# Moving the 128x64 block-mask add of an attention kernel from GpSimd to VectorE

## The chip, the cores and the metric

The kernel runs as one program on the 8 cores of one Trainium2 chip. Each core takes 2 of the 16 sequences (2048 tokens each, 1024 channels) and works for itself; the cores exchange nothing. The time is the device time of the slowest core in microseconds (us). The five engines of a core are named as in the profile: PE (TensorE, matrix multiply), DVE (VectorE), ACT (ScalarE), POOL (GpSimd) and SP (SyncE, which here only starts transfers).

## The reference

For every core: layer norm of x, then x + attention(xn) + ffn(xn). The attention is block-sparse with 32-token blocks. What matters for the change is the value that `max_vals` stands for: for each query row the largest score over those key blocks that are selected.

```
low  = Qh Kh^T * scale                       # block means, 64 x 64 per head and sequence
norm = low - row_max (+5000 near the diagonal)
hi_mask = norm >= (value of the 1024th largest)
hi   = Q K^T * scale in the selected blocks  # 32 x 32 scores each
max_vals = max over the selected blocks of hi.max(-1)
out  = (sum exp(hi)V*corr + low part) / (norms*corr + 1e-6)
```

The kernel finds the row maximum of each query row in each of the 64 key blocks (64 numbers per row), adds a table that is 0 for a selected block and hugely negative for the others, and takes the maximum of the 64. Out of it only the 1e-6 term of the denominator is scaled (`eps_all`); the exponentials themselves need no maximum.

## The kernel before, in words

Every engine executes its own list of instructions strictly in the order in which the Python code emits them; there is no scheduler. A small recorder (`Rec`) writes the lists. `emit(engine, ...)` appends an instruction, and also a wait for the previous instruction of the same engine (except on PE). For a transfer started by GpSimd this means: the next transfer is issued only when the one before has landed. `wait(engine, semaphore, value)` puts an explicit wait at that place of the list. The name `gpsimdc` stands for arithmetic on GpSimd; it shares GpSimd's one list with the transfers that GpSimd starts, but counts on a semaphore of its own (sGC; transfers count on sGP).

The first 2290 us do the layer norm, the weight transposes, the block means, the search for the threshold and the ffn. The change touches nothing there. From then on there are 8 passes, one for each pair of heads. A pass handles 4 units of work called here *chunks* (2 heads x 2 sequences), and for each it needs

- *phase A*: 64 half-steps (`emit_phaseA_half`, `u` = 0 to 63). Each is one PE matmul of 128 queries against 512 keys into a half of PSUM `pA` (or `pO`) at L762, and a DVE reduction (L773) of its 128x512 scores to 16 block maxima in `bm`. Four half-steps (`kq` = 0 to 3) fill the 64 block maxima of 128 query rows. I call these four a *quad*: 16 quads a chunk, 64 a pass, 512 in all. At the end of a quad, L786 adds the mask table `bx` (bf16) to the 64 numbers, and L791 (DVE) reduces them to one number in `mv_all`. `bx` comes by a transfer (L696, and its small companion `rmb`, L701) into one of two buffers, `bx0` or `bx1`.
- *the chunk loop* (`emit_chunk_iter`, `kg` = 0 to 31): two matmuls into `pS` (L851), the exponential on ACT from `pS` to `aT` (L866), and two matmuls of `aT` with the values into `pO` (L819), the latter one step late. Then an epilogue (L923 to L993) with two 128x1024 additions on GpSimd (L986, L989) and the store.

Phase A runs ahead of the chunk loop. A pass begins with the *V part*: 8 projection groups of the values (L1069, 8 matmuls each, into the halves of `pA`), 32 small transposes (L1098), and 20 quads between them, which use `pA` and `pO` as four slots ("wide"). The other 44 quads lie inside the chunk loops: two half-steps per `kg`, in all of the first loop, in three quarters of the second and third, and 8 `kg` of the fourth; there only the two halves of `pA` serve as slots. A half-step's matmul waits until the reduction that read the same slot last is done.

Of the kernel before, what the change touches and what calls it, by code (L numbers as in the profile page):

```python
# [12 lines left out]
ALU = mybir.AluOpType  # L13
# [82 lines left out]
def build_program(debug=False, trunc=None):  # L96
# [36 lines left out]
    with stack:  # L133
        r = Rec(nc, stack)

        def sb(name, shape, dt):
            return stack.enter_context(nc.sbuf_tensor(name, shape, dt))
# [68 lines left out]
        with contextlib.ExitStack() as st_p0:  # L206
# [135 lines left out]
            def bh_idx(p, hip, s):  # L342
                return (2 * p + hip) * 2 + s
# [293 lines left out]
        with contextlib.ExitStack() as st_p2:  # L637
# [17 lines left out]
            bmm = sb("bmm", [128, 64], F32)  # L655
            bx2 = [sb("bx0", [128, 1024], BF), sb("bx1", [128, 1024], BF)]
# [16 lines left out]
            def bh_idx(p, hip, s):  # L673
# [8 lines left out]
            state = {"ndv_ep": 0, "prev_evac": 0, "chunk_pe_end": 0,  # L682
                     "nac_la": [0, 0], "ngp_prep": [0, 0], "ndv_prep": [0, 0],
                     "ngp_bx": [0, 0], "nac_eps": 0, "ngc_mv": [0, 0],
                     "nac_la_last": 0, "ngp_prep_last": 0,
                     "prev_exp": [0, 0], "phA_dv": 0, "phA_done_dv": [0, 0], "pO_dv": 0,
                     "nst_a": 0, "ngp_rmb": [0, 0], "prev_exp2": [0, 0], "phA_dv4": [0, 0, 0, 0], "nac_ep": 0,
                     "pcons": [0, 0], "nac_qk": 0, "nsy_part": [0, 0], "ngp_add": [0, 0],
                     "nst_a2": [0, 0], "pA_free_ac": [0, 0], "pending_w1": None, "npe_vtr": 0}
# [50 lines left out]
            def emit_phaseA_half(p, hip, sq, u, wide=False):  # L740
                b = bh_idx(p, hip, sq)
                bpar = b % 2
                bmp = bm2c[bpar]
                p0 = 64 * hip
                ts0 = sq * S
                t, kq = u // 4, u % 4
                nsl = 4 if wide else 2
                sl4 = u % nsl
                pap = [pA[:, 0:512], pA[:, 512:1024],
                       pO[:, 0:512], pO[:, 512:1024]][sl4]  # L750
                r.wait("tensor", "sDV", state["phA_dv4"][sl4])
                if sl4 < 2:
                    r.wait("tensor", "sAC", state["pcons"][sl4])
                    r.wait("tensor", "sAC", state["pA_free_ac"][sl4])
                else:
                    r.wait("tensor", "sAC", state["prev_evac"])
                r.wait("tensor", "sDV", state["ndv_ep"])
                if u == 0:
                    r.wait("tensor", "sGP", state["ngp_bx"][bpar])
                    r.wait("tensor", "sAC", state["nac_qk"])  # L760
                r.emit("tensor", lambda e, p0=p0, ts0=ts0, t=t, kq=kq, pap=pap:
                       e.matmul(pap,  # L762
                                qtp[p0:p0 + 64,
                                    ts0 + t * 128:ts0 + (t + 1) * 128],
                                ktp[p0:p0 + 64,
                                    ts0 + kq * 512:ts0 + (kq + 1) * 512],
                                start=True, stop=True))
                npe_a = r.cnt["sPE"]
                r.wait("vector", "sPE", npe_a)
                if kq == 0:  # L770
                    r.wait("vector", "sGC", state["ngc_mv"][bpar])
                nred = r.emit("vector", lambda e, kq=kq, pap=pap, bmp=bmp:
                              e.tensor_reduce(  # L773
                                  bmp[:, kq * 16:(kq + 1) * 16],
                                  pap.rearrange("p (k e) -> p k e", e=32),
                                  axis=AX.X, op=ALU.max))
                state["phA_dv4"][sl4] = nred
                if sl4 >= 2:
                    state["pO_dv"] = nred
                if kq == 3:  # L780
                    r.wait("gpsimdc", "sDV", nred)
                    if u == 3:
                        r.wait("gpsimdc", "sGP", state["ngp_bx"][bpar])
                    state["ngc_mv"][bpar] = r.emit(
                        "gpsimdc", lambda e, t=t, bmp=bmp, bpar=bpar:
                        e.tensor_tensor(bmm[:, :], bmp[:, :],  # L786
                                        bx2[bpar][:, t * 64:(t + 1) * 64],
                                        ALU.add))
                    r.wait("vector", "sGC", state["ngc_mv"][bpar])
                    r.emit("vector", lambda e, b=b, t=t:  # L790
                           e.tensor_reduce(  # L791
                               mv_all[:, b * 16 + t:b * 16 + t + 1],
                               bmm[:, :], axis=AX.X, op=ALU.max))
                if u == 63:
                    r.wait("vector", "sGP", state["ngp_rmb"][bpar])
                    r.wait("vector", "sGC", state["ngc_mv"][bpar])
                    r.wait("vector", "sAC", state["nac_eps"])
                    r.emit("vector", lambda e, b=b: e.tensor_scalar(
                        epst[:, :], mv_all[:, b * 16:(b + 1) * 16],
                        0.125, None, ALU.mult))  # L800
                    ndv_e = r.emit("vector", lambda e, bpar=bpar: e.tensor_tensor(
                        epst[:, :], epst[:, :], rmb2[bpar][:, :], ALU.max))
                    r.wait("scalar", "sDV", ndv_e)
                    state["nac_eps"] = r.emit("scalar", lambda e, b=b: e.activation(
                        eps_all[:, b * 16:(b + 1) * 16], epst[:, :],
                        AF.Exp, bias=clneps[:, :]))
                    state["phA_done_dv"][bpar] = ndv_e
# [34 lines left out]
            def emit_chunk_iter(p, hip, sq, par, kg, units):  # L842
                qh, k = kg // 16, kg % 16
                kpar = kg % 2
                r.wait("tensor", "sAC", state["prev_exp"][kpar])
                if kg == 0:
                    r.wait("tensor", "sGP", state["ngp_prep"][par])
                    r.wait("tensor", "sDV", state["ndv_prep"][par])
                for sl in range(2):
                    r.emit("tensor", lambda e, k=k, qh=qh, sl=sl, par=par, bpar=kpar:  # L850
                           e.matmul(pS[bpar][:, sl * 512:(sl + 1) * 512],  # L851
                                    lhs2[par][:, k * 128:(k + 1) * 128],
                                    rhs2[par][:, qh * 1024 + sl * 512:
                                              qh * 1024 + (sl + 1) * 512],
                                    start=True, stop=True))
                npe_s = r.cnt["sPE"]
                if kg > 0:
                    emit_av(p, hip, sq, par, kg - 1)
                if kg == 4 and state["pending_w1"] is not None:
                    state["pending_w1"]()  # L860
                    state["pending_w1"] = None
                for bhu, u in units:
                    emit_phaseA_half(*bhu, u)
                r.wait("scalar", "sPE", npe_s)
                newexp = r.emit("scalar", lambda e, bpar=kpar:
                                e.activation(aT[bpar][:, :], pS[bpar][:, :],  # L866
                                             AF.Exp, scale=0.125))
                state["prev_exp2"][kpar] = newexp
                state["prev_exp"][kpar] = newexp
# [151 lines left out]
            for p in range(8):  # L1021
# [26 lines left out]
                def pre_phA():  # L1048
                    for _ in range(2):
                        if upos[0] < 80:  # L1050
                            emit_phaseA_half(*pre_units[upos[0]][0],
                                             pre_units[upos[0]][1], wide=True)
                            upos[0] += 1
# [182 lines left out]
```

How the kernel before makes its waits and increments, by code:

```python
    def emit(self, eng, fn):  # L57
        sname = ESEM[eng]
        n = 16 if eng in ("sync", "gpsimd") else 1
        if eng != "tensor" and self.cnt[sname]:
            self.wait(eng, sname, self.cnt[sname])
        self.cnt[sname] += n
        h = self.sem[sname]
        self._push(eng, lambda e, fn=fn, h=h, n=n: fn(e).then_inc(h, n))
        return self.cnt[sname]
# [1 line left out]
    def wait(self, eng, sname, val):  # L67
        if not val:
            return
        h = self.sem[sname]
        self._push(eng, lambda e, h=h, v=val: e.wait_ge(h, v))
```

## Time and profile before

| | us |
|---|---|
| median of 3 runs (lowest, highest) | 6074.62 (6059.57, 6076.16) |
| the profiled execution | 6075.57 |
| its span, slowest core (7) | 6074.0 |
| spans of the 8 cores | 6032.3 to 6074.0 |
| busy PE / DVE / ACT / POOL in the span | 3214.6 / 2371.4 / 1711.1 / 451.9 |
| the stretch of the 8 passes | 2290 to 6074 |

Busy shares are averages: no engine is busy much more than half of the span, and inside a pass the engine that the others wait for changes from part to part. Rows of the timeline have the start in us, the duration, engine, line, operation, output <- inputs, how many instructions were merged (x2), and in brackets how long the engine had been idle before and what released it. PEclk is the granted PE clock as a share of 2.4 GHz, so 0.50 is its lower level, 1.2 GHz.

### The profile page before, as it was taken

How to read it: one execution, taken by the hardware profiler on the slowest of the kernel's cores; microseconds unless marked ns; L12 is line 12 of the kernel's file. 1: busy time of each engine (PE TensorE's matmuls, PEld its weight loads, DVE VectorE, ACT ScalarE, POOL GpSimd, SP SyncE). 2: the span in 40 equal slices, each digit the busy share in tenths (PEclk: the TensorE clock that was granted, in tenths of full speed). 3: DMA queues.
4: the chain of work that ended last, by engine and by line, in shares of the span. 5: the costliest groups of instructions: out<-in, count | busy, mean ns of one | idle time of the engine just before them, and what ended most of it. 6: DMA issues, size and time to landing. Idle time of an engine off the chain costs nothing.

```text
span 6074.0 us, 58969 instructions; the slowest of 8 cores (6032.3 to 6074.0 us)
## 1 busy us (share of the span) xinstructions
PE 3214.6 (53%) x11513; PEld 1116.3 (18%) x11513; DVE 2371.4 (39%) x4751; ACT 1711.1 (28%) x2627; POOL 451.9 (7%) x813
## 2 busy tenths in 40 slices
PE   1121113333333416776676776776776676677676
PEld 0021101111111102221222122122122122122122
DVE  3421214333444223533542542542541642542543
ACT  2200000000000002452443353354354254245245
POOL 0000010000000000110110110011011011010011
PEclk9965556677666856886887787787687688688678
DMA  2234001121111210111110100111011010010011
GB/s 62 66 75 78 2 16 41 43 49 44 40 42 40 60 41 16 22 21 20 22 22 11 29 16 19 21 22 20 17 27 20 16 27 18 18 27 18 11 20 21
DMA packets 516791, 181.80 MB, mean 30 GB/s; under 512 B 494282, under 2 KB 495474, under 8 KB 516274
## 3 DMA queue, kind: packets, MB, share of 16 engines
q1 hardware_dynamic: 482386, 130.46, 9.4%
q0 software_dynamic: 34080, 47.56, 4.3%
q8 instruction: 135, 2.21, 0.2%
q14 instruction: 190, 1.56, 0.1%
HBM read 142.23 MB, written 39.34 MB: 30 GB/s over the span
## 4 chain that ended last, share of the span: by engine, by line
PE 33%; DVE 20%; DMA 20%; issue 12%; ACT 12%; POOL 1%; DVEq 1%; ACTq 0%; POOLq 0%; SPq 0%
DVE bm L773 8%; PE pS L851 8%; PE pO L819 7%; PE pA L762 6%; ACT aT L866 6%; PE pA L1008 3%; DMA bx<-bsm_dram 3%; PE pA L516 3%; DMA fW<-wT_r 3%; DMA fW<-wT_k 3%; ACT stage L947 2%; PE pA L1069 2%; DMA fW<-wT_v 2%; DMA nb<-norm_all 2%; DVE fA L501 2%
## 5 line engine op out<-in xcount | busy, mean ns | idle before, releaser
L773 DVE TENSOR_REDUCE bm<-pA 128x16 f32<-128x512 f32 x1728 | 1194.8, 691 | 766.0 <-PE pA L762 627.4
L866 ACT ACTIVATE aT<-pS 128x1024 bf16<-128x1024 f32 x1024 | 1049.3, 1025 | 870.7 <-PE pS L851 827.1
L762 PE MATMUL pA<-ktp,qtp 64*128 64x512 bf16 x1728 | 724.7, 435 | 507.2 <-DVE bm L773 118.3
L819 PE MATMUL pO<-aT,vtm 128*65 128x512 bf16 x2048 | 717.4, 437 | 321.0 <-ACT aT L866 318.7
L851 PE MATMUL pS<-rhsc,lhsc 128*128 128x512 bf16 x2048 | 727.9, 445 | 0.1
L516 PE MATMUL pA<-fA,fW 128*128 128x512 bf16 x1536 | 417.5, 425 | 283.7 <-DMA fW<-wT_r 80.1
L417 PE MATMUL pB<-bis_cnt,ones 128*128 128x32 f32 x116 | 35.2, 397 | 684.4 <-DVE bis_cnt L413 684.4
L762 PEld LDWEIGHTS pA<-ktp,qtp 64*128 64x128 bf16 x1728 | 157.9, 95 | 1116.1 <-issue 1111.1
L819 PEld LDWEIGHTS pO<-aT,vtm 128*65 128x65 bf16 x2048 | 238.5, 125 | 666.5 <-issue 524.9
L786 POOL TENSOR_TENSOR bmm<-bm,bx 128x64 f32<-128x64 f32 x512 | 155.5, 304 | 2196.8 <-DVE bm L773 2196.6
L1069 PE MATMUL pA<-xnT,wsl_v 128*128 128x512 bf16 x512 | 189.8, 537 | 220.5 <-DMA out<-stage 131.0
L773 DVE TENSOR_REDUCE bm<-pO 128x16 f32<-128x512 f32 x320 | 221.2, 691 | 157.1 <-PE pO L762 126.8
L791 DVE TENSOR_REDUCE mv_all<-bmm 128x1 f32<-128x64 f32 x512 | 112.5, 220 | 435.3 <-POOL bmm L786 435.3
L516 PEld LDWEIGHTS pA<-fA,fW 128*128 128x128 bf16 x1536 | 152.3, 106 | 543.6 <-issue 434.1
L547 ACT ACTIVATE fR<-pA 128x512 bf16<-128x512 f32 x64 | 38.2, 598 | 683.6 <-PE pA L516 683.5
L851 PEld LDWEIGHTS pS<-rhsc,lhsc 128*128 128x128 bf16 x2048 | 161.0, 107 | 328.5 <-issue 291.9
L762 PE MATMUL pO<-ktp,qtp 64*128 64x512 bf16 x320 | 172.5, 559 | 20.5 <-ACT vtm L1109 2.5
L581 ACT ACTIVATE fA<-fB 128x512 bf16<-128x512 bf16 x64 | 40.4, 631 | 478.3 <-DVE fB L574 473.2
L547 ACT ACT_TABLE_LOAD x1 | 1.3, 1283 | 604.0 <-PE pA L516 604.0
L417 PEld LDWEIGHTS pB<-bis_cnt,ones 128*128 128x128 f32 x116 | 29.1, 311 | 693.4 <-issue 693.4
L1008 PE MATMUL pA<-xnT,wsl_q 128*128 128x512 bf16 x512 | 121.8, 384 | 65.2 <-DMA wsl_v<-wT_v 63.7
L1077 ACT ACTIVATE vTf<-pA,bcol_v 128x512 bf16<-128x512 f32 x64 | 44.1, 689 | 367.0 <-PE pA L1069 366.9
(150 smaller groups left out, 2523.2 us busy)
## 6 DMA issues: line engine op xcount, KB each, us to landing
xtile<-x SPq DMA_DIRECT2D x64, 512.0 KB
fW<-wT_r SPq DMA_DIRECT2D x64, 256.0 KB
fW<-wT_k SPq DMA_DIRECT2D x64, 256.0 KB
fW<-wT_v SPq DMA_DIRECT2D x64, 256.0 KB
out<-stage SPq DMA_DIRECT2D x32, 512.0 KB
rhsc<-qtp POOLq DMA_DIRECT2D x32, 256.0 KB, 3.6
lhsc<-ktp POOLq DMA_DIRECT2D x32, 256.0 KB, 2.9
bx<-bsm_dram POOLq DMA_DIRECT2D x32, 256.0 KB, 8.1
```

The lines of the kernel that those rows point to most:

```text
L501: e.scalar_tensor_tensor(d[:, c * QT:(c + 1) * QT], xnT[:, base:base + QT], mucol[m][:, c:c + 1], d[:, c * QT:(c + 1) * QT], ALU.mult, ALU ...
L516: e.matmul(pA[:, sl * 512:sl * 512 + QT], w[:, cc * 128:(cc + 1) * 128], rb[:, cc * QT:(cc + 1) * QT], start=(cc == 0), stop=(cc == 7)))
L762: e.matmul(pap, qtp[p0:p0 + 64, ts0 + t * 128:ts0 + (t + 1) * 128], ktp[p0:p0 + 64, ts0 + kq * 512:ts0 + (kq + 1) * 512], start=True, stop ...
L773: e.tensor_reduce(bmp[:, kq * 16:(kq + 1) * 16], pap.rearrange("p (k e) -> p k e", e=32), axis=AX.X, op=ALU.max))
L786: e.tensor_tensor(bmm[:, :], bmp[:, :], bx2[bpar][:, t * 64:(t + 1) * 64], ALU.add))
L791: e.tensor_reduce(mv_all[:, b * 16 + t:b * 16 + t + 1], bmm[:, :], axis=AX.X, op=ALU.max))
L819: e.matmul(pO[0:65, sl * 512:(sl + 1) * 512], vtm[:, (sq * 16 + k) * 130 + hip * 65: (sq * 16 + k) * 130 + hip * 65 + 65], aT[bpar][:, sl ...
L851: e.matmul(pS[bpar][:, sl * 512:(sl + 1) * 512], lhs2[par][:, k * 128:(k + 1) * 128], rhs2[par][:, qh * 1024 + sl * 512: qh * 1024 + (sl + ...
L866: e.activation(aT[bpar][:, :], pS[bpar][:, :], AF.Exp, scale=0.125))
L947: e.activation(stg[:, i * 64:(i + 1) * 64], pA[:, sl8 * 128:sl8 * 128 + 64], AF.Identity, scale=rdenw16[:, i:i + 1])))
L1008: e.matmul(pA[:, slot * 512:(slot + 1) * 512], wsl[tag][:, cc * 128:(cc + 1) * 128], xnT[:, cc * T + n * 512:cc * T + (n + 1) * 512], star ...
L1069: e.matmul(pA[:, slot * 512:(slot + 1) * 512], wsl["v"][:, cc * 128:(cc + 1) * 128], xnT[:, cc * T + n * 512: cc * T + (n + 1) * 512], sta ...
```

## The change

The mask addition of every quad is emitted on DVE in place of GpSimd. With it go GpSimd's wait for the fourth reduction, DVE's wait for GpSimd, and, since the number kept in `ngc_mv` is now 0 and a wait for 0 is not emitted, the two other DVE waits on it. The explicit wait for the mask table at `u == 3` goes too; PE already waits for the same transfer before the chunk's first half-step (`u == 0`), and DVE for PE.

```
                 if kq == 3:
-                    r.wait("gpsimdc", "sDV", nred)
-                    if u == 3:
-                        r.wait("gpsimdc", "sGP", state["ngp_bx"][bpar])
-                    state["ngc_mv"][bpar] = r.emit(
-                        "gpsimdc", lambda e, t=t, bmp=bmp, bpar=bpar:
-                        e.tensor_tensor(bmm[:, :], bmp[:, :],
-                                        bx2[bpar][:, t * 64:(t + 1) * 64],
-                                        ALU.add))
-                    r.wait("vector", "sGC", state["ngc_mv"][bpar])
+                    r.emit("vector", lambda e, t=t, bmp=bmp, bpar=bpar:
+                           e.tensor_tensor(bmm[:, :], bmp[:, :],
+                                           bx2[bpar][:, t * 64:(t + 1) * 64],
+                                           ALU.add))
+                    state["ngc_mv"][bpar] = 0
```

On DVE, in the first quad of a pass (`pA`, `pO` are the PSUM slots, `bm` the block maxima, `bmm` their masked copy), the list had

```order
L773 TENSOR_REDUCE bm<-pA 128x16 x2
L773 TENSOR_REDUCE bm<-pO 128x16 x2
L791 TENSOR_REDUCE mv_all<-bmm 128x1
L773 TENSOR_REDUCE bm<-pA 128x16 x2
L773 TENSOR_REDUCE bm<-pO 128x16 x2
```

and has now (lines from here on are 4 lower in the changed kernel)

```order
L773 TENSOR_REDUCE bm<-pA 128x16 x2
L773 TENSOR_REDUCE bm<-pO 128x16 x2
L782 TENSOR_TENSOR bmm<-bm,bx 128x64
L787 TENSOR_REDUCE mv_all<-bmm 128x1
L773 TENSOR_REDUCE bm<-pA 128x16 x2
```

Each quad has one more instruction on DVE, ahead of the last reduction.

On GpSimd, from the start of a pass to the middle of its first chunk loop (`rhsc`, `lhsc` are the chunk's operands, `bx0`, `bx1` the mask buffers), the list had

```order
L710 DMA rhsc<-qtp 64x2048
L712 DMA lhsc<-ktp 64x2048
L696 DMA bx0<-bsm_dram 128x1x1024
L701 DMA rmb0<-rm_dram 128x1x16
L696 DMA bx1<-bsm_dram 128x1x1024
L701 DMA rmb1<-rm_dram 128x1x16
L786 TENSOR_TENSOR bmm<-bm,bx0 128x64 x16
L786 TENSOR_TENSOR bmm<-bm1,bx1 128x64 x4
L710 DMA rhsc1<-qtp 64x2048
L712 DMA lhsc1<-ktp 64x2048
L786 TENSOR_TENSOR bmm<-bm1,bx1 128x64 x8
L696 DMA bx0<-bsm_dram 128x1x1024
```

and has now

```order
L696 DMA bx1<-bsm_dram 128x1x1024
L701 DMA rmb1<-rm_dram 128x1x16
L710 DMA rhsc1<-qtp 64x2048
L712 DMA lhsc1<-ktp 64x2048
L696 DMA bx0<-bsm_dram 128x1x1024
L701 DMA rmb0<-rm_dram 128x1x16
L710 DMA rhsc<-qtp 64x2048
L712 DMA lhsc<-ktp 64x2048
```

No addition stands behind a transfer any more, and the transfers of `bx` and `rmb` in the first chunk loop stand right behind those of `rhsc1` and `lhsc1`.

## Rows read from the trace of the kernel before

**Rows 1.** Windows: one pass; PE, PEld, DVE, ACT, POOL busy, PEclk, DMA share, GB/s.

```profile
3283.00:3756.00 473.00, 326.47 (x1072) 102.50 (x1072) 202.28 (x360) 193.19 (x296) 49.33 (x88) 0.78 0.10 20
```

**Rows 2.** Groups by line: busy us, mean ns | idle before, releaser.

```profile
L786 POOL TENSOR_TENSOR bmm<-bm,bx 128x64 f32<-128x64 f32 x512 | 155.5, 304 | 2196.8 <-DVE bm L773 2196.6
L791 DVE TENSOR_REDUCE mv_all<-bmm 128x1 f32<-128x64 f32 x512 | 112.5, 220 | 435.3 <-POOL bmm L786 435.3
```

**Rows 3.** Timeline, V part, end of one quad.

```profile
3291.71 1.49 DVE L773 TENSOR_REDUCE bm<-pO 128x16 f32<-128x512 f32 x2
3293.88 0.22 DVE L791 TENSOR_REDUCE mv_all<-bmm 128x1 f32<-128x64 f32 x1 [0.68 <-POOL bmm L786]
3294.20 1.49 DVE L773 TENSOR_REDUCE bm<-pA 128x16 f32<-128x512 f32 x2
```

**Rows 4.** Timeline, first chunk loop, PE and DVE around the end of a quad.

```profile
3399.63 0.37 PE L762 MATMUL pA<-ktp,qtp 64*128 64x512 bf16 x1 [0.35 <-issue]
3400.18 1.49 DVE L773 TENSOR_REDUCE bm<-pA 128x16 f32<-128x512 f32 x2 [0.21 <-PE pA L762]
...
3400.43 0.37 PE L762 MATMUL pA<-ktp,qtp 64*128 64x512 bf16 x1 [0.42 <-ACT aT L866]
...
3401.70 0.80 PE L762 MATMUL pA<-ktp,qtp 64*128 64x512 bf16 x2
...
3402.35 0.22 DVE L791 TENSOR_REDUCE mv_all<-bmm 128x1 f32<-128x64 f32 x1 [0.68 <-POOL bmm L786]
...
3402.67 1.49 DVE L773 TENSOR_REDUCE bm<-pA 128x16 f32<-128x512 f32 x2
```

**Rows 5.** Windows of line L791 alone: DVE busy (x count), PEclk.

```profile
3289.00:3376.00 87.00, 4.17 (x19) 0.56 0.09 19
3393.00:3463.00 70.00, 3.08 (x14) 0.83 0.03 5
3490.00:3540.00 50.00, 2.64 (x12) 0.95 0.08 17
3649.00:3662.00 13.00, 0.88 (x4) 1.00 0.19 32
```

**Rows 6.** Timeline, first chunk loop at the lower PE clock.

```profile
3444.68 1.06 PE L819 MATMUL pO<-aT,vtm 128*65 128x512 bf16 x2
...
3447.47 1.06 PE L819 MATMUL pO<-aT,vtm 128*65 128x512 bf16 x2
```

**Rows 7.** Groups by line on DVE: two-input additions and products.

```profile
L426 DVE TENSOR_TENSOR bis_lo<-bis_t,bis_lo 128x32 f32<-128x32 f32 x58 | 11.1, 192 | 6.0
...
L731 DVE TENSOR_TENSOR la_t<-la_t 64x64 f32<-64x64 f32 x32 | 6.9, 217 | 4.0 <-DVE la_t L728 1.0
```

**Rows 8.** Timeline, start of a pass, around its first quad.

```profile
3272.57 1.90 PE L1069 MATMUL pA<-xnT,wsl_v 128*128 128x512 bf16 x8
...
3275.66 0.81 PE L762 MATMUL pA<-ktp,qtp 64*128 64x512 bf16 x2 [1.20 <-ACT vTf L1077]
3280.21 0.68 POOL L701 DMA_DIRECT2D rmb<-rm_dram  x1 [7.75 <-DMA bx<-bsm_dram]
...
3281.39 0.22 DVE L791 TENSOR_REDUCE mv_all<-bmm 128x1 f32<-128x64 f32 x1 [7.32 <-POOL bmm L786]
3281.72 1.49 DVE L773 TENSOR_REDUCE bm<-pA 128x16 f32<-128x512 f32 x2
3283.35 3.57 PE L1069 MATMUL pA<-xnT,wsl_v 128*128 128x512 bf16 x8 [6.87 <-DVE bm L773]
```

**Rows 9.** Timeline, first chunk loop, around its second mask transfer.

```profile
3425.10 0.22 DVE L791 TENSOR_REDUCE mv_all<-bmm 128x1 f32<-128x64 f32 x1 [4.95 <-POOL bmm L786]
...
3426.60 0.58 PE L762 MATMUL pA<-ktp,qtp 64*128 64x512 bf16 x1 [3.70 <-DVE bm L773]
```

**Rows 10.** Timeline, second chunk loop: last stage addition, next phase A reduction.

```profile
3483.15 2.12 POOL L989 TENSOR_TENSOR stage<-stage,vTf 128x1024 f32<-128x1024 f32 x1
...
3486.95 1.49 DVE L773 TENSOR_REDUCE bm<-pA 128x16 f32<-128x512 f32 x2 [10.82 <-PE pA L762]
```

## The prediction

> **What bounds the kernel now.** I read the view of the cores first (their spans lie within 0.7%, so core 7 speaks for all), then the windows, the groups by line, and the timeline of one pass. The passes repeat with a period of about 473 us [rows 1], and eight of them fill the 3784 us after 2290 us. In one, PE is busy 326 us and DVE 202 us of 473: neither is full, so the question is who waits for whom in each part.
>
> The groups by line name the exchange that the change removes. DVE sits idle 435.3 us in all ahead of the 512 L791 reductions, always for GpSimd's addition [rows 2]. That is 0.85 us each, where the addition itself lasts 0.304 us. Only idle time of an engine that the others wait for is worth anything, so I looked where DVE is that engine.
>
> *V part.* One quad ends with two reductions that start at 3291.71 and take 1.49 us, then 0.68 us idle, then L791 for 0.22 us, then the next reduction at 3294.20 [rows 3]. A quad is four reductions (2 x 1.49), the wait, L791 and gaps of about 0.1 us: 1.49 + 0.10 + 1.49 + 0.68 + 0.22 + 0.10 = 4.08 us. DVE has no idle time in it but the 0.68. The next reduction starts 0.10 us after L791 and names no releaser, so its matmul was there: DVE sets the pace.
>
> *Chunk loops at the upper clock.* There a reduction waits 0.21 us for its matmul once in a quad [rows 4], and that matmul had waited for the slot's previous reduction, which makes a closed chain: 4.08 + 0.21 or so, less rounding, 4.19 us a quad. The row of the matmul at 3400.43 gives ACT as what released it. I don't follow this: a phase A matmul waits for the reduction of its slot (and for older ACT work), never for the last exponential; the reduction and the exponential merely end within 0.1 us of each other, and the label goes to the later. The first matmul pair of the next quad runs from 3401.70 [rows 4], so its first half is written at about 3402.1 and could be read 0.18 us later, at 3402.28 (as the one at 3399.63, over at 3400.00, is read at 3400.18); the reduction starts at 3402.67, after L791. DVE is late by 0.39 us. This 0.39 us is what can be gained here before PE becomes the bound.
>
> *Chunk loops at the lower clock.* From one L819 pair to the next it is 3447.47 - 3444.68 = 2.79 us for each `kg` [rows 6], so 5.57 us for the two `kg` of a quad, with the matmuls back to back. PE is the bound, and DVE waits. Nothing is gained in these.
>
> **The change, part by part.**
>
> *The round trip in quads that DVE paces.* Removed: 0.68 us idle. Added: the addition on DVE and one more gap, since every DVE instruction waits for the one before. The trace has no 128x64 addition on DVE. Near it are one of 64x64 with 217 ns and one of 128x32 with 192 ns; 6.0 us idle before 58 of the latter is 0.10 us a gap [rows 7]. It is the length in a partition that counts, and that is 64, so I take 0.22 us. From the last reduction to L791 it will then be 0.10 + 0.22 + 0.10 = 0.43 us (unrounded gaps of 0.105), and the saving 0.25 us a quad. Bounds: 0.19 us for the addition saves 0.28; 0.304, what it takes on GpSimd, saves 0.17. Both are under the 0.39 us of slack found above, so in the chunk loops PE doesn't take over; 0.14 us of slack is left.
>
> How many quads: the four windows of L791 hold 19, 14, 12 and 4 [rows 5]; the third chunk loop repeats the second, with 12. In the V part 2 of 19 lie in the stretch of projections where PE leads. In the first loop 4 of 14 fall at the lower clock or behind the stall below. In the second and third I drop 2 each for the same reason. That leaves 17 + 10 + 10 + 10 + 4 = 51; I count 50 a pass, 400 in all. 400 x 0.25 = 100 us. With 42 a pass at 0.17 us it would be 57 us, with 60 at 0.28 us 134 us.
>
> *The addition's place behind transfers.* GpSimd's list has the `rmb1` transfer, which waits for `bx1` to land, ahead of the first quad's addition. So L791 waits 7.32 us at 3281.39, though its data were there, and the next projection group starts only at 3283.35, after a PE idle time of 6.87 us [rows 8]. Without the wait: the matmul pair starts at 3275.66 in any case (it waits for ACT), its first half is there at about 3276.06, the two reductions run from 3276.24 to 3277.73, and the group starts 0.14 us after (as 3283.35 stands to the end of the reductions at 3283.21), at 3277.87. Saved: 5.48 us. The same happens in the first loop: L791 waits 4.95 us for an addition behind `bx0` and `rmb0`, and PE 3.70 us for the reductions behind it [rows 9]. I take the 3.70. What is late next is PE itself, which has its `pS` and `pO` work ready. Together 9.18 us a pass, 73 us over 8. This pass is typical: 435.3 - 512 x 0.68 = 87.1 us of longer waits in all [rows 2] is 10.9 a pass, and here it is 6.64 + 4.27 = 10.9. Bounds 60 and 80 us, as the waits of other passes may differ in how much PE loses.
>
> *The clock after these stalls.* The projection group before the stall took 1.90 us for 8 matmuls, the one behind it 3.57 us [rows 8]: the clock had fallen to its lower level over 6.87 us without work. If PE pauses only about 1.4 us there, it may keep the upper level, and up to 1.7 us more is saved. In the first loop the lower level before and behind the 3.70 us pause may end earlier, worth up to 0.7 us for each `kg` (2.79 against 4.19/2), two `kg` at most. So 0 to 3.1 us a pass; I take 1, 8 us in all, with 0 and 25 as ends. The Trainium skill says the same of direction (TensorE: Matmul & The Clock Gate, "What's actually happening": the throttled state is the default and activity releases it). By this rule a shorter pause can only help; by it the term would be at its upper end, and the trace agrees so far as a 1.90 us group turned into a 3.57 us group behind the pause.
>
> *The transfers.* GpSimd now issues `bx0` for the third chunk right behind the first loop's `rhsc1` and `lhsc1`, some 25 us earlier, once the first chunk's phase A is done. Nobody waits for it earlier or later; DMA is 10% busy [rows 1]. Nothing.
>
> *GpSimd beside DVE.* The additions left on GpSimd are the stage additions. The last of a pair ends at 3485.27, the next phase A reduction starts at 3486.95 [rows 10], and its quad ends later still, so they don't meet. Nothing. The Trainium skill warns here (GPSIMD Engine Reference, "Specifications": GpSimd shares its SBUF interfaces with VectorE and contends with VectorE instructions that have two SBUF inputs). The new addition is just such an instruction. No row shows it beside GpSimd work; the rival on it is below.
>
> **Sum**, against the profiled execution (6075.6 us, span 6074.0, median of the runs 6074.6, so nothing to correct): 100 + 73 + 8 = 181 us less, **5895 us**. The ends of the terms give 57 + 60 + 0 = 117 and 134 + 80 + 25 = 239: 5959 to 5837.
>
> **The rivals.**
>
> *The chunk loops are paced by ACT after all*, as the releaser in rows 4 says. Then 33 of the 50 quads give nothing: 17 x 8 x 0.25 = 34, plus 73, is 107 us: 5969. Against it stands that the matmul starts 0.42 us after the reduction's end in every such row whatever the exponential does.
>
> *The clock helps more*: the first loop has 0.83 where the later ones reach 0.95 and 1.00 [rows 5]. If it rises to theirs, some 10 us a pass change level, at (2.79 - 2.1)/2.79 of their time: 2.5 us a pass more than the ends above allow in that loop: 20 us, 5875 or, with high ends elsewhere, 5840.
>
> *Contention of DVE and GpSimd*: if the adds slide into the 2.34 and 2.12 us stage additions and wait for them, 4.46 us for each of 32 pairs is 143 us against the 181: 6037. Against it: the gap in rows 10, and that both move together.
>
> *Slower*: the PE clock in the chunk loops. PE is at the upper level there only while it is busy enough; a new cadence of pauses, or another phase of them, could keep it at the lower one. Each quad of the loops would then take 5.57 in place of 4.19 us. All 33 x 8 = 264 quads at the lower level cost 264 x 1.38 = 364 us, the V part and the stalls give back 107: 6332. It decides against the change from 181/(1.38 + 0.25) = 111 quads on. Against it: the change makes PE's pauses shorter everywhere. The addition alone can't bring slower: it would have to take 0.47 us to eat its own gain, and 0.65 us to eat the stalls' too (73/400 = 0.18 more), against 0.22 for its neighbours.
>
> *That it doesn't do what it says* would be an addition that still waits for a transfer. The order shows none.
>
> **How the numbers follow.** Forecast 70%, more clock 11%, ACT-paced loops 11%, contention 4%, slower 3%, and 1% for no change at all. The range of 8 in 10 takes the ends of the terms and most of the first two rivals: 5840 to 5965. A measurement of this kernel can tell 0.3%, 18 us, from no change; faster than that are all but the last two cases and a small part of contention: 0.95 faster, 0.02 same, 0.03 slower.
>
> **What would show it.** Right: L791 (now L787) has no wait of its own over 0.12 us; a quad of the V part takes 3.83 us and one in the loops 3.94 us at the upper clock; the new addition 0.22 us; the projection group at the start of a pass waits under 2 us; no PE pause over 3 us in the middle of the first loop; a pass takes about 450 us. Wrong: quads of 4.19 us in the loops (ACT paces), an addition of over 0.3 us or some of several us (contention), or a mean PEclk in the passes under the 0.78 of before (the clock). The 2290 us ahead of the passes should not change.

## The result, and the profile after

| | before | changed |
|---|---|---|
| median of 8 runs, us | 6063.1 | 5845.8 |
| lowest, highest | 6059.5, 6076.2 | 5839.0, 5864.1 |
| profiled execution, us | 6075.6 | 5854.1 |
| span of its slowest core | 6074.0 (core 7) | 5852.5 (core 6) |

The ratio is 0.9643 (95% interval 0.9627 to 0.9658), so 216 us less, with 207 to 226 as the interval. Forecast were 181, within 117 to 239 by the ends of the terms; the median lies 6 us above the lower end of the range given for the time (5840 to 5965).

The groups by line of the changed kernel, where [rows 2] had 435.3 us of idle time ahead of L791 (busy us, mean ns | idle before):

```profile
L782 DVE TENSOR_TENSOR bmm<-bm,bx 128x64 f32<-128x64 f32 x512 | 115.5, 225 | 54.2 <-DVE bm L773 1.4
L787 DVE TENSOR_REDUCE mv_all<-bmm 128x1 f32<-128x64 f32 x512 | 112.3, 219 | 54.5 <-DVE bmm L782 2.8
```

The 435.3 us have become two idle times of 54 us (0.106 each, the gap of any two DVE instructions) and 115.5 us of work: 0.225 us an addition, where 0.22 was forecast. A quad of the V part, from the timeline, against [rows 3]:

```profile
3230.49 0.22 DVE L787 TENSOR_REDUCE mv_all<-bmm 128x1 f32<-128x64 f32 x1
3230.82 1.49 DVE L773 TENSOR_REDUCE bm<-pA 128x16 f32<-128x512 f32 x2
3232.40 1.49 DVE L773 TENSOR_REDUCE bm<-pO 128x16 f32<-128x512 f32 x2
3233.99 0.23 DVE L782 TENSOR_TENSOR bmm<-bm,bx 128x64 f32<-128x64 f32 x1
3234.32 0.22 DVE L787 TENSOR_REDUCE mv_all<-bmm 128x1 f32<-128x64 f32 x1
```

From L787 to L787 it is 3.83 us, where it was 4.08. A quad of the first chunk loop at the upper clock, against [rows 4]:

```profile
3328.48 0.22 DVE L787 TENSOR_REDUCE mv_all<-bmm 128x1 f32<-128x64 f32 x1
3328.80 1.49 DVE L773 TENSOR_REDUCE bm<-pA 128x16 f32<-128x512 f32 x2
...
3330.51 1.49 DVE L773 TENSOR_REDUCE bm<-pA 128x16 f32<-128x512 f32 x2 [0.22 <-PE pA L762]
...
3330.75 0.37 PE L762 MATMUL pA<-ktp,qtp 64*128 64x512 bf16 x1 [0.42 <-ACT aT L862]
...
3332.03 0.80 PE L762 MATMUL pA<-ktp,qtp 64*128 64x512 bf16 x2
3332.10 0.23 DVE L782 TENSOR_TENSOR bmm<-bm,bx 128x64 f32<-128x64 f32 x1
3332.43 0.22 DVE L787 TENSOR_REDUCE mv_all<-bmm 128x1 f32<-128x64 f32 x1
3332.75 1.49 DVE L773 TENSOR_REDUCE bm<-pA 128x16 f32<-128x512 f32 x2
```

3.95 us, where it was 4.19. The last reduction still follows L787 by 0.10 us with no releaser, so DVE still paces this stretch, though the row of the matmul at 3330.75 still names ACT. That the name is wrong can be counted. In the kernel before, 189 of the 222 such rows start 0.46 us after the end of the slot's reduction; in the changed one it is 221 of 276, at 0.46 us again. The distance to the end of the last exponential moved meanwhile from mostly 0.40 us to mostly 0.16 us. (The 0.42 us in the brackets is the time that PE had been idle.) The start of a pass, against [rows 8]:

```profile
3220.18 0.81 PE L762 MATMUL pA<-ktp,qtp 64*128 64x512 bf16 x2 [1.20 <-ACT vTf L1073]
3220.73 1.49 DVE L773 TENSOR_REDUCE bm<-pA 128x16 f32<-128x512 f32 x2 [1.50 <-PE pA L762]
3222.36 1.89 PE L1065 MATMUL pA<-xnT,wsl_v 128*128 128x512 bf16 x8 [1.37 <-DVE bm L773]
3223.80 0.68 POOL L701 DMA_DIRECT2D rmb<-rm_dram  x1 [7.53 <-DMA bx<-bsm_dram]
```

The projection group no longer waits for `bx1` (the `rmb1` issue behind its landing comes at 3223.80, after the group's start), and takes 1.89 us here, not 3.57. This pass is a good one: over the 8 passes of this core the group takes 1.89, 2.78, 1.89, 1.89, 2.61, 1.89, 2.26 and 3.23 us, over all 64 passes of the 8 cores 2.31 us in the mean, against 3.55 before.

**Where the time went, by pieces.** The evacuations of `pO` to `outT` (two in each chunk) cut a pass into 8 pieces that hold the same work in every variant. Pieces 1 to 7 are chunk loops; the last runs through the V part to the middle of the first loop, and is listed first below. Beside each length stands the time at the lower PE clock: 2 x (1 - PEclk) x length, from the windows of each piece, mean of 8 passes and 8 cores, in us (7 passes for the first row, since no evacuation precedes the first pass).

| piece | before: length, lower clock | changed: length, lower clock |
|---|---|---|
| V part and first half of loop 1 | 178.2, 124.5 | 166.1, 115.5 |
| second half of loop 1 | 46.5, 22.2 | 39.2, 9.8 |
| first half of loop 2 | 41.4, 16.0 | 40.3, 14.5 |
| second half of loop 2 | 41.0, 8.9 | 38.4, 5.5 |
| first half of loop 3 | 41.5, 17.2 | 40.5, 15.3 |
| second half of loop 3 | 36.1, 4.5 | 33.5, 0.3 |
| loop 4, two halves | 84.4, 17.4 | 83.4, 18.7 |
| a pass | 469.1, 210.5 | 441.3, 179.5 |

27.8 us a pass, 222 in eight. The forecast had 22.6. It was not only waits that went: 31 us a pass less stand at the lower clock. In one pass the second half of loop 1, before and changed, is

```profile
3415.04:3462.31 47.27, 35.04 (x96) 8.92 (x94) 24.11 (x42) 17.73 (x18) 3.72 (x10) 0.75 0.05 6
```

```profile
3344.63:3383.26 38.63, 29.19 (x96) 8.20 (x94) 25.82 (x49) 17.70 (x18) 0.00 (x0) 0.91 0.00 1
```

(window, length; busy PE, PEld, DVE, ACT, POOL; PEclk, DMA share, GB/s). The same 96 matmuls need 29.2 us of PE in place of 35.0.

**A granted clock of 0.81.** The sum above takes the clock as either 0.50 or 1.00. In four of the profiles some cores also show 0.81, between the two levels. In the changed kernel, in the passes, these are cores 6 and 7 alone, from 4926 us on. On core 6, whose profile is shown:

```profile
4926.50:4954.00 27.50, 25.03 (x96) 10.20 (x94) 0.00 (x0) 14.70 (x17) 0.00 (x0) 0.81 0.00 1
```

```profile
4922.50 1.89 PE L1004 MATMUL pA<-xnT,wsl_q 128*128 128x512 bf16 x8
4927.93 2.28 PE L1004 MATMUL pA<-xnT,wsl_k 128*128 128x512 bf16 x8
```

The two whole passes with it take 449 to 450 us on these two cores, where the others take 442 to 446. In the table it adds 1.0 us to the 179.5 of the changed kernel (178.5 are at the lower level itself), and nothing to the kernel before, which never shows it. The second execution of the changed kernel (e9) doesn't show it either. In e5 it weighs more, see there.

### The profile page after: what moved, and what is told of

It is laid out like the page before. It is cut to its first block, busy times and chain, and to the rows that moved or that the text cites. A ratio compares the mean times of both kernels' runs of the same rounds, so it can differ in the third digit from the quotient of the medians.

```text
span 5852.5 us, 57371 instructions; the slowest of 8 cores (5818.4 to 5852.5 us)
## 1 busy us (share of the span) xinstructions
PE 3152.6 (54%) x11513; PEld 1107.5 (19%) x11513; DVE 2487.2 (42%) x5263; ACT 1706.9 (29%) x2627; POOL 286.8 (5%) x301
## 4 chain that ended last, share of the span: by engine, by line
PE 35%; DVE 21%; DMA 17%; ACT 14%; issue 11%; DVEq 1%; ACTq 1%; POOL 0%; SPq 0%; POOLq 0%
PE pS L847 8%; DVE bm L773 8%; ACT aT L862 8%; PE pA L762 7%; PE pO L815 6%; PE pA L1004 3%; PE pA L516 3%; DMA fW<-wT_r 3%; PE pA L1065 3%; ACT stage L943 2%; DMA fW<-wT_v 2%; DMA nb<-norm_all 2%; DVE fA L501 2%; DMA fW<-wT_k 2%; DVE bis_ge L409 1%
## 5 line engine op out<-in xcount | busy, mean ns | idle before, releaser
L762 PE MATMUL pA<-ktp,qtp 64*128 64x512 bf16 x1728 | 710.6, 421 | 399.1 <-ACT aT L862 117.8
L815 PE MATMUL pO<-aT,vtm 128*65 128x512 bf16 x2048 | 692.3, 423 | 312.1 <-ACT aT L862 311.5
L847 PE MATMUL pS<-rhsc,lhsc 128*128 128x512 bf16 x2048 | 707.6, 434 | 0.1
L762 PEld LDWEIGHTS pA<-ktp,qtp 64*128 64x128 bf16 x1728 | 159.3, 95 | 995.6 <-issue 991.7
L762 PE MATMUL pO<-ktp,qtp 64*128 64x512 bf16 x320 | 172.3, 559 | 19.7 <-DVE bmm L782 4.1
L581 ACT ACTIVATE fA<-fB 128x512 bf16<-128x512 bf16 x64 | 40.3, 629 | 475.5 <-DVE fB L574 470.4
L943 ACT ACTIVATE stage<-pA,rdenw 128x64 f32<-128x64 f32 x384 | 120.5, 314 | 67.6 <-DVE rdenw L933 33.9
L782 DVE TENSOR_TENSOR bmm<-bm,bx 128x64 f32<-128x64 f32 x512 | 115.5, 225 | 54.2 <-DVE bm L773 1.4
```

The source lines that it names most:

```text
L762: e.matmul(pap, qtp[p0:p0 + 64, ts0 + t * 128:ts0 + (t + 1) * 128], ktp[p0:p0 + 64, ts0 + kq * 512:ts0 + (kq + 1) * 512], start=True, stop ...
L782: e.tensor_tensor(bmm[:, :], bmp[:, :], bx2[bpar][:, t * 64:(t + 1) * 64], ALU.add))
L815: e.matmul(pO[0:65, sl * 512:(sl + 1) * 512], vtm[:, (sq * 16 + k) * 130 + hip * 65: (sq * 16 + k) * 130 + hip * 65 + 65], aT[bpar][:, sl ...
L847: e.matmul(pS[bpar][:, sl * 512:(sl + 1) * 512], lhs2[par][:, k * 128:(k + 1) * 128], rhs2[par][:, qh * 1024 + sl * 512: qh * 1024 + (sl + ...
L943: e.activation(stg[:, i * 64:(i + 1) * 64], pA[:, sl8 * 128:sl8 * 128 + 64], AF.Identity, scale=rdenw16[:, i:i + 1])))
```

## The experiments

All are compared with the kernel before, run on the same chip. Differences to the changed kernel (0.9643) are of the ratios times 6063 us.

**1 and 2: put one stall back.**

```
  # e1, ahead of the DVE addition
+ if wide and b % 4 == 0 and u == 3:
+     r.wait("vector", "sGP", state["ngp_bx"][1])
  # e2
+ if not wide and b % 4 == 1 and u == 51:
+     r.wait("vector", "sGP", state["ngp_bx"][0])
  # e2, ahead of emit_prep_bx(*bhs[2]) at kg == 16
+ r.wait("gpsimd", "sDV", r.cnt["sDV"])
```

> The changed kernel, with one wait put back: DVE waits, ahead of the addition of the first quad of each pass, for the landing of the second mask table (bx1), as GpSimd's list order made it wait before. Theory A (the stall costs its wait and the PE clock behind it): 5.5 us a pass for the wait and 1.7 us for the next projection group, which falls back from 1.9 to 3.6 us: 8 x 7.2 = 57 us more than the changed kernel's 5846, so 5903 (ratio to the kernel before 0.974). Theory B (only the wait counts, the clock term is nothing): 44 us, 5890 (0.971). If the later DVE-paced quads absorbed it, it would be 5846 (0.964).

Measured: 0.9698 (0.9681 to 0.9714), 5878 us, 33 us over the changed kernel. DVE's restored waits are shorter than those they stand for, since DVE waits for the landing only and not for GpSimd's next issue too: 36.6 us for eight, where L791's first waits of the eight passes were 53.2. One of them:

```profile
3215.68 0.23 DVE L784 TENSOR_TENSOR bmm<-bm,bx 128x64 f32<-128x64 f32 x1 [3.63 <-DMA bx<-bsm_dram]
...
3217.96 3.47 PE L1067 MATMUL pA<-xnT,wsl_v 128*128 128x512 bf16 x8 [3.06 <-DVE bm L773]
```

PE's extra pause is 3.06 - 1.37 = 1.7 here, and 4.42 - 1.37 = 3.05 in the next pass (DVE wait 4.54), so 1.5 to 1.9 us less than DVE's wait. For the mean wait of 4.6 that is 2.9 us, 23 us in all. The group takes 3.46 us in the mean of all cores and passes where the changed kernel has 2.31, which is 9 more. 32 for 33 measured: theory A in kind, scaled to the shorter wait. The total could not tell it from the 23 us of the wait alone (the difference is known to some 14 us); that the clock has a part in it is read from the group's duration.

> The changed kernel, with the other stall put back: in each first chunk loop GpSimd issues the third chunk's mask transfer only at kg 16 and DVE's addition of the quad u = 51 waits for its landing. Theory A (the wait of 3.7 us and in addition a longer stretch at the lower PE clock; the piece from the first to the second evacuation of pO shrank by 7.5 us a pass, of which the quads explain 1.3): 6.2 x 8 = 50 us more than 5846, so 5896 (0.972). Theory B (only the 3.7 us): 30 us, 5876 (0.969).

Measured: 0.9714 (0.9698 to 0.9731), 5890 us, 43 us over the changed kernel. The waits are only 22.7 us for eight here (37.0 in the kernel before), 2.8 each. But the piece is 4.8 us longer (44.0 for 39.2), with 9.8 us more at the lower clock. Its row in the pass that corresponds:

```profile
3356.24:3398.49 42.25, 31.98 (x94) 8.70 (x94) 25.84 (x49) 17.71 (x18) 1.43 (x2) 0.84 0.05 7
```

In the trace PE's idle time ahead of that matmul is 1.0 to 3.6 us, 2.35 in the mean of this core's eight, of which 0.4 is usual. So about 60% of this stall's price is the clock behind it (9.8 x 0.3 = 2.9 us, with the price worked out below), and 1.9 us the wait. Theory A. The 43 us alone, with some 14 us of uncertainty for a difference of two ratios, would not rule out B's 30. The other loop pieces have another 6 us a pass more at the lower clock than in the changed kernel (2.9 of it in the second half of loop 2), though their quads are as short.

What does the lower clock cost? e1, e2 and the changed kernel have the very same instructions in the second half of loop 2, and nothing there was touched. The lengths are 38.98 (e1), 39.38 (e2) and 38.39 us (changed kernel), with 7.40, 8.58 and 5.54 us at the lower clock. 0.99 us for 3.04 (e2 against the changed kernel) is 0.33 us for each us. In the second half of loop 3 it is 33.79 against 33.46 for 1.79 against 0.27: 0.22. I use 0.3, an estimate. [rows 6] and the 4.19 us quad give (2.79 - 2.1)/2.79 = 0.25.

**3: the addition twice.**

```
  r.emit("vector", ... e.tensor_tensor(bmm, bmp, bx2[...], ALU.add))
+ r.emit("vector", ... e.tensor_tensor(bmm, bmp, bx2[...], ALU.add))
```

> The changed kernel with the addition of every quad emitted twice (the same result written twice), which lengthens DVE's part of a quad by 0.225 + 0.105 = 0.33 us. Theory A (DVE paces 50 quads a pass, in the V part and in the chunk loops at the upper clock): 400 x 0.33 = 132 us more than 5846, so 5978 (0.986). Theory B (ACT or PE pace the chunk loops): only 17 quads a pass, 45 us: 5891 (0.972).

Measured: 0.9925 (0.9906 to 0.9944), 6013 us, 171 us over the changed kernel. Theory B (the loops paced by ACT or PE) would give 45: it falls. But 171 is also more than A's 132. The seven pieces of loops have 80.1 us at the lower clock in place of 64.1: 16 x 0.3 x 8 = 38 us, and 132 + 38 = 170. That fits, but it can't fix both the number of quads and the price of the clock.

**4: the addition on DVE in the V part only.**

```
  if kq == 3:
+     if wide:   # on DVE, as in the changed kernel
+     else:      # on GpSimd, as in the kernel before
```

> The kernel before with the addition on DVE only in the V part (20 of the 64 quads of a pass); in the chunk loops it stays on GpSimd. Theory A (my sum): 17 x 8 x 0.25 = 34 us for the quads, 44 us for the first stall, up to 13 us for the clock of the projection group behind it: 78 to 91 us less than before, 5985 to 5972 (0.987 to 0.985). Theory B (what the forecast missed, 36 us, lies in the V part): 115 us or more, 5948 or less (0.981).

Measured: 0.9860 (0.9843 to 0.9876), 5976 us, 85 us under the kernel before. It is what the forecast gave the V part (78 to 91). So what was missed lies in the loops: 216 - 85 = 131 us there, where the forecast had 66 for the quads, 30 for the stall and at most 8 for the clock. The time at the lower clock agrees: 86.3 us in the seven loop pieces of this kernel, 86.1 before, 64.1 in the changed one.

**5 to 8: what paces now.** e5 takes the masked maximum for four quads at once; e6 also moves the wait for the mask table from PE's first matmul of a chunk to DVE's first addition; e7 is the changed kernel with ACT's small exponential of a finished phase A emitted one `kg` later; e8 has all three.

```
  # e5: bm 128x256, bmm = bm
- if kq == 3:            # bx2[...][t*64:(t+1)*64], mv_all[t:t+1]
+ if kq == 3 and t % 4 == 3:   # bx2[...][(t-3)*64:(t+1)*64], mv_all[t-3:t+1]
  # e6
- if u == 0: r.wait("tensor", "sGP", state["ngp_bx"][bpar])
+ if t == 3: r.wait("vector", "sGP", state["ngp_bx"][bpar])
  # e7: after the exponential of the next emit_chunk_iter
- r.wait("scalar", "sDV", ndv_e); state["nac_eps"] = r.emit("scalar", ...)
+ state["pend_eps"] = [2, eps_fn]
```

> The changed kernel with the masked maximum taken once for four quads: one 128x256 addition (in place) and one reduction to 128x4 in place of four of each, on DVE. By the lengths of the 64-wide ones and 192 more elements at DVE's pace, about 0.42 us each, so 1.05 us with gaps for four quads against 2.62: 0.39 us a quad. Theory A (DVE paces the V part with 1.5 us of slack behind it, but in the chunk loops PE takes over after 0.14 us): 17 x 8 x 0.39 = 53 us less than the changed kernel's 5846, so 5793 (ratio to the kernel before 0.956). Theory B (the chunk loops gain the 0.14 too, or some lower-clock time goes): 90 us less, 5756 (0.950). If the lump of 1 us every fourth quad stops PE, nothing in the loops or a loss: 5800 to 5820.

Measured: 0.9591 (0.9567 to 0.9615), 32 us under the changed kernel (known to some 17): between A (53) and no gain, and within the 5800 to 5820 us expected if the lump stops PE. The two instructions take what was thought:

```profile
L783 DVE TENSOR_TENSOR bm<-bm,bx 128x256 f32<-128x256 f32 x128 | 54.5, 426 | 14.0 <-DVE bm L774 0.9
L788 DVE TENSOR_REDUCE mv_all<-bm 128x4 f32<-128x256 f32 x128 | 53.8, 420 | 13.6 <-DVE bm L783 0.5
```

The piece with the V part shrank by 5.7 us a pass (46 us in all). In the loops PE took over, as the 0.14 us of slack said, which the timeline shows with DVE now waiting 0.59 us for a matmul:

```profile
3414.38 0.37 PE L762 MATMUL pA<-ktp,qtp 64*128 64x512 bf16 x1
...
3417.01 1.49 DVE L774 TENSOR_REDUCE bm<-pA 128x16 f32<-128x512 f32 x2 [0.59 <-PE pA L762]
3418.16 0.37 PE L762 MATMUL pA<-ktp,qtp 64*128 64x512 bf16 x1
...
3420.30 0.42 DVE L783 TENSOR_TENSOR bm<-bm,bx 128x256 f32<-128x256 f32 x1
...
3422.51 0.37 PE L762 MATMUL pA<-ktp,qtp 64*128 64x512 bf16 x1 [0.51 <-DVE bm L774]
```

3.78 us for a quad without the lump and 4.35 for one with it: (3 x 3.78 + 4.35)/4 = 3.92 is no gain on 3.95. And by the formula of the table the loop pieces had 10.9 us a pass more at the lower clock than in the changed kernel. They grew by 1.5 us a pass, 12 us in all, which took back part of the 46.

Part of this is the granted clock of 0.81. Cores 0 to 3 of the profiled execution show it for 3 to 21 us a pass in the loop pieces, cores 4 to 7 never in the passes, and the slowest core (3) is one of the first four. On cores 4 to 7 a pass takes 435.5 us, against 440.9 on the six cores of the changed kernel without it: 5.4 us, 43 in eight passes, nearer to A than the 32. Their loop pieces still have 9 us a pass more at the lower level itself (73.0 against 64.0), at almost the same length (275.7 against 275.1). Why lumps do that the runs don't tell.

> As e5_batch4, and the wait for the mask table bx moves from PE ahead of a chunk's first half-step to DVE ahead of its first masked addition (after 16 half-steps). PE idles about 5.5 us a pass there now. Theory A: the V part starts by that much earlier, 8 x 5.5 = 44 us less than e5_batch4 (ratio lower by 0.007). Theory B (the later transfers, or DVE at its first addition, take it back): no change from e5_batch4.

Measured: 0.9497 (0.9481 to 0.9514), 57 us under e5: theory A. The V piece shrank by 5.3 us a pass, 42 us in all. What is more than A's 44 is within the uncertainty (some 17 us), and without the cores that show 0.81 a pass goes from 435.5 to 430.3 us, 42 us in eight.

> The changed kernel with ACT's small exponential of a finished chunk's phase A (L800, it waits for DVE and stands ahead of the chunk loop's next exponential in ACT's list) emitted one kg later, where its data have long been there. Three times a pass ACT is stopped 4.5 us there in place of its usual 1.4, and PE pauses over 3 us, behind which the PE clock is at its lower level. Theory A (pauses cost their length and the lower clock behind them): 3 x 8 x 3.0 = 72 us, and some 8 us less at the lower level each time, at 0.3 us per us (as pieces of equal instructions in the runs so far show) 24 x 2.4 = 58 us: 130 us less than 5846, 5716 (0.943). Theory B (the clock costs nothing): 72 us, 5774 (0.952). Theory C (DVE paces these loops anyway and catches up in the pause): under 20 us, 5830 (0.962).

Measured: 0.9532 (0.9518 to 0.9546), 67 us under the changed kernel. That is B's 72 by size, though not as B has it, and half of A's 130: the three pieces with such a pause shrank by 4.0, 4.3 and 1.9 us, with 10.1 us less at the lower clock (worth 3), so the pauses gave 7 us, and two other pieces grew by 0.7 each, with 1.9 and 2.9 us more at the lower clock. The clock I had expected behind each pause (8 us) was 3. ACT's idle time ahead of that exponential fell from 167.6 us to 4.6:

```profile
L803 ACT ACTIVATE eps_all<-epst,clneps x32: 307/308/309, 2411.1 to 5726.0; 128x16 f32<-128x16 f32 x32
its engine sat idle before it (us, times) until:
  DVE epst L797: 4.6, 8
```

> e6_batch4_bxwait and e7_eps_later together, the fastest version that the runs point to. If they add up as each theory A has it: 53 + 44 + 130 = 227 us less than 5846, 5619 (0.927). If PE becomes the bound in the loops and the clock gain is shared: about 5680 (0.937).

Measured: 0.9360 (0.9345 to 0.9376), 5662 us, the fastest version here, between the two expectations: 172 us under the changed kernel, where e6 (89) and e7 (67) alone add to 156. By the length of a pass, without the cores that show 0.81, the parts add up: 10.6 us (e6) and 8.4 (e7) less than 440.9, and 19.7 with both.

**9: the changed kernel again.**

> The changed kernel itself a second time, for how far the share of the lower PE clock is a property of the kernel or of one execution. In the first profiled execution the seven pieces between evacuations of pO outside the V part had 64 us a pass at the lower clock (mean of 8 cores), the kernel before 86, and the runs with one stall put back 71 and 80. Theory A (the kernel sets it): 60 to 68 us again, and the ratio to the kernel before again 0.963 to 0.966. Theory B (chance of the execution): anything from 64 to 80 us, and then the differences of under 10 us between variants mean nothing.

Measured: 0.9646 (0.9620 to 0.9671). 65.9 us a pass at the lower clock in the seven loop pieces, 64.1 the first time. So differences of 10 us and more between variants are not the chance of one execution, and those of 2 us can be. This was tried for one kernel only. (The 71 us named in the expectation for one of the runs with a stall is 68.0 for e1, by the same windows as in the table.)

## Why the prediction was right, point by point

**Quads that DVE paces: right.** 0.25 us was forecast for one and 4.08 - 3.83 and 4.19 - 3.95 are measured, the addition takes 0.225 us, the slack of 0.14 us in the loops was real (e5). The count of 50 a pass was somewhat high. From one L791 to the next, 41 intervals a pass are under 4.35 us in the kernel before, and 44 from one L787 to the next are under 4.10 us in the changed one (means of the 8 cores), 14 of them in the V part. By these 82 to 88 us stand, not 100. e3's 171 us go with 50 quads too, but only with a price for the clock that is itself an estimate. Where I had written "4.08 + 0.21 or so", the sum is 4.29: the 0.21 us stand in place of the usual gap of 0.10, which gives the 4.19. The reading against the profile's label (ACT) was right as well, though the distance to the reduction's end is 0.46 us, not 0.42.

**The two stalls: right in kind, the size of one pass taken for all.** At the start of a pass PE was forecast at 3277.87 in place of 3283.35; measured is a pause of 1.37 us where 1.4 was forecast. The 73 us came from one pass with long waits (7.32 and 4.95). The eight first waits sum to 53.2 us and the eight in the loop to 37.0; less the 1.84 and 1.25 us by which PE's loss is shorter, that is 38 + 27 = 65 us. PE's own idle times bear this out: over eight passes of the same core they fall by 37 us at the start of the pass, and are 28 us behind the stall in the loop. I had written that this pass was typical by the sum of its waits over 0.68 us, 10.9 us. That sum had been shared out to these two waits alone; in the mean of the eight passes they have 9.9, and the rest is spread over other quads, thirteen of which wait 1.03 us.

**The clock: the term that was mis-sized.** Forecast were 8 us, with 0 and 25 as ends. The step was "the clock after these stalls", as though only the two stalls moved the clock, and by two `kg` at most. The projection group did three quarters of what was said (2.31 for 3.55 us in the mean, 1.24 us a pass, 10 us). But the seven loop pieces lost 22 us a pass at the lower clock, of which 12.4 in the second half of loop 1, behind the stall there, and the rest (9.6) mostly in the second halves of loops 2 and 3, where no stall was. The shorter quads can do that: e3, with nothing but longer quads, has 16 us a pass more in the loops. The stall can too: e2, with only the stall put back, has 10 us more in its own piece and 6 in those behind. So how much of the 22 belongs to which is not shown: each of these two puts back 16 of the 22. e4 shows that both lie in the loops: with the additions of the V part alone moved, the loops stay at 86.3. 22 x 0.3 x 8 = 53 us. Together 63 us, not 8, and far above the 25 that I had as its upper end. That the total fell into the range in spite of it is partly luck: the quads and the stalls came out 20 us or more smaller than forecast.

82 to 88 + 65 + 63 is 210 to 216 where 216 (207 to 226) are measured and 222 by the pieces. The slope of 0.3 is known to some 0.08, which is 14 us of the 63, so the sum closes no better than that. That the clock term is several times the forecast doesn't hang on it: e3 shows the same share with the other sign, with nothing changed but DVE's pace, and e2 shows it behind one stall.

I had also weighed the Trainium skill (TensorE: Matmul & The Clock Gate, "What's actually happening": activity releases the throttle) and written that by it the term would be at its upper end. For this change the trace agrees in direction, with 31 us a pass less at the lower clock; the size was above that end. It isn't enough as a rule for what comes next: in e5 PE's idle times of over 0.4 us sum to 55.6 us a pass in the loops of the profiled core, against 57.1 in the changed kernel, and yet it has more time at the lower clock.

**GpSimd beside DVE: right, since they don't meet.** The new addition takes 224 to 227 ns in all its instances, 512 on each core of the changed kernel, and none of them overlaps with an addition on GpSimd. So the warning of the Trainium skill (GPSIMD Engine Reference, "Specifications") was not put to the test; no run here shows what an overlap would cost.

**Signs that I named.** A pass of 450 us: it is 441. PEclk over 0.78: 0.80 by the pieces. The stretch ahead of the passes unchanged: the first L762 starts at 2315 us before and after, in the mean of the cores. L787 without a wait over 0.12 us: ten of 512 have 0.23 to 0.46 us. No PE pause over 3 us in the middle of the first loop: wrong as a sign, since another pause of 3.25 us lies there, behind ACT's small exponential; it was there before the change too, and e7 removes it. I had not looked for what else stopped PE in that piece.

**The rivals.** ACT-paced loops fall with e3 and the 3.95 us; contention with the additions never meeting; slower with the result. "The clock helps more", given 11%, is what came on top of the forecast, with 55 us more than the term's 8, where it had 20.

## What to carry to other kernels

- A small operation handed to another engine in the middle of a chain costs its round trip (0.68 us here for 0.30 us of work), and it also stands in that engine's list behind whatever waits for a transfer. Done on the engine that has the data it cost 0.33 us here and waited for nobody. Look at both: the median wait gives the first, the few long waits the second.
- Where PE's clock moves between its levels, a saving elsewhere can be worth more than the time it takes off the chain, and a delay can cost more (e2, e3). It is not sure: e5 saved time on DVE and had more time at the lower clock. Cut the trace into pieces of equal work and put the time at the lower level beside each length; two variants with the same instructions in a piece give its price. Look also for cores with a third value of the clock before a difference of some 20 us is explained.
- Before crediting a removed wait with all its length, list every wait of that kind, and look what else stops the waiting engine in the same place.

## What the runs showed of the hardware

- The time at the lower PE clock repeated from one execution to another of the same kernel: 64.1 and 65.9 us a pass in the loop pieces in two executions, against 86.1 (before), 80.0 (e2), 80.1 (e3) and 75.0 (e5) in others. It changed in pieces with identical instructions when something well ahead of them was altered: the second half of loop 2 has 5.5 us in the changed kernel, 8.6 in e2, whose stall is 75 us earlier, and 7.4 in e1, whose stall is 206 us earlier. What carries it over that distance stays open.
- A release label can name the wrong engine for hundreds of rows: ACT was named for PE's matmul in phase A, whose wait was for DVE. The constant 0.46 us from the end of the reduction tells it, while the distance to the exponential changed with the kernel.
- A granted clock of 0.81 shows in stretches on some cores: 6 and 7 of the changed kernel in the passes, 0 to 3 of e5, 4 and 5 of e6. Eight 128x512 matmuls take 2.28 us at it, 1.89 at 1.00 and 3.57 at 0.50. It came with one execution of the changed kernel and not with the other, so it is not the kernel's alone; what brings it on is not shown.
- A 128x64 addition with one bf16 operand takes 0.225 us on DVE, a 128x256 one 0.426 us: 1.05 ns an element and 0.16 us fixed.
